# Attention steps on TensorE: the scores of the next two steps issued in front of the projections' parts instead of behind them

## The reference

```
xn = _layernorm(x, axis=-1)
x = x + _L0_attn_ref(xn, w_qkv, w_out) + _L0_ffn_ref(xn, wg, w1, b1, w2, b2)
...
scores = jnp.einsum('bhnqd,bhnkd->bhnqk', qb, k_kv) * scale      # 16 heads of 16, blocks of 64 queries x 128 keys
scores = jnp.where(_band_mask(nb), scores, NEG_INF)
attn = jax.nn.softmax(scores, axis=-1)
ob = jnp.einsum('bhnqk,bhnkd->bhnqd', attn, v_kv)
out = ob...reshape(B, L, D) @ w_out
```

## Time and profile before

| | |
|---|---|
| three runs | 757.99, 759.27, 761.73 us, median 759.27 |
| the profiled execution | 760.58 us, span 758.8 us |
| granted TensorE clock, mean | 0.949 of full speed |
| PE, PEld busy | 93%, 80% |
| DVE, ACT, POOL busy | 63%, 63%, 56% |
| attention | 461 to 759 us |

### The profile page before, as it was taken

The page is one execution under the profiler, slowest core; times in us unless marked ns, Lnnn a source line. Parts: engine busy times, 40 slices in busy tenths (PEclk is TensorE's granted clock), DMA queues, the critical chain, the costliest instruction groups (busy, mean ns, idle before and its releaser), DMA issues. The chain is left out here.

```text
span 758.8 us, 18403 instructions
## 1 busy us (share of the span) xinstructions
PE 705.8 (93%) x5816; PEld 603.4 (80%) x5817; DVE 481.7 (63%) x1774; ACT 480.2 (63%) x1508; POOL 427.7 (56%) x818
## 2 busy tenths in 40 slices
PE   6686799999999999999999997999999999999885
PEld 3364689898898988989889896788888878878664
DVE  7773243543425345253452524999999989999994
ACT  4640480834709357192561905998989989999891
POOL 4502560543605336153351303899999989999993
PEclk8875699999999999999999998999999999999897
DMA  9722231142311423123241013132333415141411
GB/s 314 277 77 77 87 104 58 62 138 83 110 56 60 140 76 114 54 74 125 76 124 42 0 43 108 35 91 85 96 96 85 121 53 141 37 120 36 115 57 42
DMA packets 52308, 69.95 MB, mean 92 GB/s; under 512 B 6672, under 2 KB 44816, under 8 KB 52240
## 3 DMA queue, kind: packets, MB, share of 16 engines
q1 hardware_dynamic: 45744, 52.31, 21.3%
q0 software_dynamic: 6144, 16.79, 8.0%
q10 hardware_dynamic: 352, 0.04, 0.0%
HBM read 47.75 MB, written 16.78 MB: 85 GB/s over the span
## 5 line engine op out<-in xcount | busy, mean ns | idle before, releaser
L1059 ACT ACTIVATE a_p<-a_p,a_nmax 128x128 f32<-128x128 f32 x512 | 198.6, 395 | 35.6 <-DVE a_nmax L1088 35.4
L990 POOL TENSOR_SCALAR a_p<-a_p,a_rsum 128x128 f32<-128x128 f32 x512 | 192.3, 391 | 18.8 <-DVE a_rsum L1096 16.5
L719 DVE TENSOR_TENSOR m_hl<-m_hf,m_hh 128x512 fp32r<-128x512 f32 x128 | 93.1, 727 | 100.3 <-ACT m_hh L676 100.3
L55 PE MATMUL m_psY<-m_w2h,m_hh 128*128 128x256 f32 x512 | 145.1, 283 | 0.0
L55 PE MATMUL m_psY<-m_w2l,m_hh 128*128 128x256 f32 x512 | 143.8, 281 | 0.0
L55 PE MATMUL m_psY<-m_w2h,m_hl 128*128 128x256 f32 x512 | 143.8, 281 | 0.0
L672 ACT ACTIVATE m_hf<-m_psF,b1T 128x512 f32<-128x512 f32 x128 | 88.4, 691 | 66.3 <-PE m_psF L55 52.1
L640 POOL CAST m_w2h<-raw 128x256 fp32r<-128x256 f32 x64 | 25.4, 396 | 175.8 <-PE m_psY L55 120.5
L1088 DVE CUSTOM_DVE_ANT_0 a_p<-a_psS,mask 128x128 f32<-128x128 f32 x512 | 116.6, 281 | 6.3 <-PE a_psS L1212 5.1
L55 PE MATMUL m_psF<-m_xh,w1h 128*128 128x512 f32 x256 | 103.6, 405 | 1.9 <-DVE m_xl L696 1.9
L55 PE MATMUL m_psF<-m_xh,w1l 128*128 128x512 f32 x256 | 102.1, 399 | 0.0
(11 more groups left out here) (186 smaller groups left out, 1363.1 us busy)
## 6 DMA issues: line engine op xcount, KB each, us to landing
raw<-in_L_ffn_w SPq DMA_DIRECT2D x16, 1024.0 KB, 5.3
y_scratch<-y SPq DMA_DIRECT2D x64, 128.0 KB, 1.7
n_xin<-in_L_attn_x SPq DMA_DIRECT2D x8, 512.0 KB, 7.4
xn_scratch<-n_xn SPq DMA_DIRECT2D x8, 512.0 KB, 7.6
a_res<-in_L_attn_x SPq DMA_DIRECT2D x8, 512.0 KB, 3.8
out<-a_res SPq DMA_DIRECT2D x8, 512.0 KB, 3.0
xnr<-xn_scratch SPq DMA_DIRECT2D x7, 512.0 KB, 5.1
b2b<-in_L_ffn_b SPq DMA_DIRECT2D x8, 128.0 KB, 4.8
```

The source lines that it names most:

```text
L55: last = pe.matmul(out, a, b, start=(n_start and i == 0), stop=(n_stop and i == n - 1))
L719: dve.tensor_tensor(hl[:, u // HC, u % HC, :], hf[:, u % FR, :], hh[:, u // HC, u % HC, :].bitcast(fp32), ALU.subtract).then_inc(hl_done, 1)
L990: pool.tensor_scalar(e, e, rsum[:, r, j:j + 1], 0.0, ALU.mult, ALU.add).then_inc(norm_done, 1)
L1059: act.activation(e, e, ACT.Exp, scale=-1.0, bias=nmax[:, r, j:j + 1], accum_out=sums[:, r, j:j + 1]).then_inc(exp_done, 1)
```

## The change

In `steps` of PE the two lines that issue the scores of steps t+2 and t+3 move from behind the projections' parts to in front of them. Nothing else changes; no instruction is added or removed, and the order on DVE, ACT, POOL and SP is the same as before.

```diff
                         ins.then_inc(pv_done, 1)
+                    if t % 2 == 0 and (t < BS - 2 or t == BS - 2 and not last):
+                        scores(b, t + 2, first)
                     if t < BS:
                         for i in range(NI):
                             parts = [part for item, part in parts_at[t % STEPS] if item == i]
...
                                 product(kind, j, 1 - u, count(b, u, i, first, last), i % 2,
                                         16 * (b * 2 + u + 2), (b * 2 + u) * (STEPS // GRP), parts)
-                    if t % 2 == 0 and (t < BS - 2 or t == BS - 2 and not last):
-                        scores(b, t + 2, first)
```

## The result

The changed kernel takes 782.71 us (median of 4, 780.97 to 784.49) against 760.50 (median of 4 of the kernel before, 757.99 to 763.94): a ratio of 1.029 with a 95% interval of 1.027 to 1.031. It is slower by 22 us; 777 was forecast, with a range of 766 to 791. The profiled execution takes 780.97 us, the shortest of the four, with a span of 779.2 us against 758.8.

A forecast was written before the change was run, and what follows sets the result against it. DVE and PE were both taken as full in the steady part, each idle moment on DVE adding time. 2.45 us in each of seven units gave 17.2, ramp and last unit zero: 777 us, range 766 to 791.

The forecast's parts named there:

- the clock's rival: New PE waits of 1.1 to 1.2 us make the granted clock fall once per unit: 787 us, chance 0.25.
- DVE has nothing to gain and pays each wait: Steady part: DVE does not wait for scores, so earlier ones win nothing; every idle moment put on DVE adds time.
- x, 0.4: Step 0: scores wait for DVE's last maximum, so x0 reaches ACT and DVE's a_xTl 0.4 us late per unit.
- k0, 0.3: Steps 2 to 4: k0's parts land behind the scores of step 4, and DVE reads k 0.3 us late.
- q1, 1.0: Steps 5 to 8: ACT gets q1 1.1 us late, and its exps delay DVE's reciprocal of step 8 by 1.0.
- v0, 0.45, and v2, 0.3: Steps 12 to 16: ACT reads v0 1.1 to 1.2 us late; 0.45 passes to DVE's reciprocal, v2 adds 0.3.
- o, nothing: Steps 8 to 11: DVE reads o one step later and is itself 1.7 us late, so no loss.
- The ramp, 0, between -2.3 and +3: First unit: gain from fewer DVE waits and loss from later q0 and k0, left at zero, bounds -2.3 to +3 us.
- Switching between kinds of tiles: Transposes directly before scores cost up to 0.23 us more in even steps: 0.3 per unit, 779; left out of the sum.
- Half of the walk: ACT and DVE run ahead in places and the reciprocal's wait is not reached: 1.2 us per unit, 768, chance 0.11.
- a shift paid once: PE falls behind DVE by one wait of 0.5 to 1.1 us, then never waits again: 760 us, chance 0.05.
- faster: Earlier scores feed a starved chain in the ramp and last unit: at most 3.7 us gained, 755.6, chance 0.04.

The follow-up runs named there:

- e4: Kernel before, with scores moved in front of the parts in steps 2, 8 and 10 alone: 770.83 us, ratio to before 1.0028.
- e1: Kernel before, with scores moved in front of the parts in step 6 of each unit alone: 773.89 us, ratio to before 1.0063.
- e5: Changed kernel, with ACT reading q1, v0 and v2 behind the step's exps instead of in front: 780.76 us, ratio to the kernel before 1.0160.
- e3: Kernel before, with scores moved in front of the parts in steps 0 and 4 alone: 776.22 us, ratio to before 1.0092.
- e10: Changed kernel, with the old order put back in step 2 of each unit: 790.30 us, ratio to the kernel before 1.0316.
- e12: e11 plus eight matmuls, their result overwritten, in front of the scores of step 12 to fill PE's wait: 775.21 us, ratio to the kernel before 1.0112.
- e2: Kernel before, with scores moved in front of the parts in steps 12 and 14 alone: 783.06 us, ratio to before 1.0176.
- e11: e2 run once more as the reference for e12: 780.41 us, ratio to the kernel before 1.0189.

## Why the prediction was right

The direction and the mechanism held, and the size in the main. The sum was 17.2 + 0 and the measured difference of the profiled spans is 20.4: 3.2 of the 5.7 us between 777 and 782.7. The other 2.5 come from the step to the median, for which the forecast took 1.3 off, rounded up by 0.5, while the median of the changed kernel lies 1.7 above its profiled execution. Their mean granted clocks are 0.947 (profiled), 0.947, 0.941 and 0.945, so some of that may be clock; no trace shows where.

Two things were luck. Within the unit the misses at x (0.4 too much) and q1 (0.4 too little) cancel, which is why 2.45 lies so near the measured 2.7. And by its number alone 782.7 is nearer to the clock's rival, 787, than to 777; it is the trace, with a granted clock of 1.00 in the units, that decides between them.

*DVE has nothing to gain and pays each wait.* Shown: the unit grew by 2.8 and DVE's idle time by 2.4 of it; e4 shows no gain from early scores in the steady units; e1 shows the loss where PE has no wait before the scores; e5 shows that 9.5 us of the loss go when ACT's order protects the reciprocal.

*x, 0.4.* Measured 0. The walk took DVE as punctual at step 0, but the reciprocal of step 0 is already 0.52 late, which covers it. Here one delay hides the next on the same engine. e3 shows it from the other side: its reciprocal of step 0 is on time, and DVE stands 0.36 before a_xTl, released by ACT, in three of its units (0.16 in two others), close to the 0.4 of the walk.

*k0, 0.3.* Measured 0.27.

*q1, 1.0.* Measured 1.41, the largest mis-sized term in the unit. The 0.96 on ACT before q1 is less than the 1.1 forecast, but the walk left out what ACT lost before it: 0.19 at q0 and 0.33 at the product with v, which had become late too. ACT had no room to make these up. Its three waits are 1.48 in all, DVE's two up to this reciprocal 0.27 + 1.41 = 1.68. The walk was right that the way from step 4's scores decides; my later theory of step 2 (e10) was not.

*v0, 0.45, and v2, 0.3.* Measured 0.51 and 0.52, with ACT 1.19 late at v0 where 1.1 to 1.2 was forecast; e12 has 0.52 and 0.54 with these steps alone.

*o, nothing.* DVE has no wait before a_res in the unit.

*The ramp, 0, between -2.3 and +3.* Measured +3.8 (6.5 less 2.7), outside these bounds, and the largest mis-sized term of the whole sum. DVE's waits there, 458 to 480 us, name it:

```profile
DVE a_p L1088 <- PE a_psS L1212: 3.8, 2, 2.7
...
DVE a_xTl L1070 <- ACT a_xTh L1017: 3.2, 2, 3.0
...
DVE a_pT L1103 <- PE a_psP L1226: 2.1, 1, 2.1
DVE a_k L1075 <- PE a_psA L1185: 1.5, 1, 1.5
```

The waits for x, transposed weights and k were 0.7, 0.9 and 0.5 before: 4.7 more. DVE's waits for scores fell from 5.1 to 3.8, the gain that the forecast had in mind, and the rest, 3.4, is most of the 3.8. x was made while PE waited for the first maxima anyway; now it comes behind them, at a lower clock (0.63 against 0.81 over the 18 us), and q0 behind it. I had the loss in mind and set it to zero for want of a row.

*Switching between kinds of tiles.* Four transposes before the scores take 0.53, the pair that no row of before showed:

```profile
594.95 0.60 PE L1226 MATMUL a_psP<-eye,a_p 128*128 128x128 f32 x4
595.48 1.16 PE L1212 MATMUL a_psS<-a_k,a_q 32*128 32x128 f32 x16
```

That is 0.17 above the 0.36 before parts. The bound of 0.23 from the v product was read from transposes that stood behind scores, so it holds two switches. Where the transposes stand behind parts, as after the change, they take the same 0.53 before the v product:

```profile
588.36 0.60 PE L1226 MATMUL a_psP<-eye,a_p 128*128 128x128 f32 x4
588.89 0.43 PE L1246 MATMUL a_psO<-a_pT,vs 128*32 128x128 f32 x8
```

The rule of the Trainium skill (page TensorEngine Tiling (Array Packing), section Key Properties) that changing the mode drains the engine agrees with it; on the way from step 4's scores to q1 the new pair lies once, in step 6.

*The rivals.* The clock did not fall in the changed kernel's steady part, so 787 was not reached, yet its mechanism is real: e2 has a fall in each of seven units and e11 in four. "Half of the walk" is refuted by the reciprocals, "a shift paid once" by units of 37.4 us one after another, "faster" by the steady units of e4. (e4's first unit is 34.0 us from x to x, against 34.5 before; with one trace of each that is not a measured gain.)

What stays open is what makes the clock fall. The length of the wait alone does not decide it: e11 loses the clock behind 1.27 and keeps it behind 1.30 and 1.33, with the same instructions in the same order. The changed kernel (both its traces) waits 1.25 in step 12 of six units and keeps it each time; it also has another wait of about 0.45 five microseconds earlier, which e2 and e11 lack, but no run varied that.

## What to carry to other kernels

Before an instruction is moved up an in-order queue, look at what it waits for, and count everything that now stands behind that wait: the instruction's own length plus the wait is added to each of them, and those whose readers have no room set the loss. Room is read between a reader's start and its producer's end, and on an engine that is full it is nothing. A delay can hide behind one that came just before it on the same engine, as x did, and small ones on the engine in between add up, as q0 and the product with v did on ACT; so walk them in order. A wait that you see grow may be a result: e5 halved PE's waits without touching PE.

## What the runs showed of the hardware

A wait of PE of 1.1 to 1.3 us can cost more than its length. In e2 and e11, 11 of 14 such waits were followed, 1 to 2 us after their end, by some 3.5 us at a granted clock of 0.50, at a price of 1.5 us per unit; three of 1.23 to 1.33 were not. With eight matmuls for nothing in its place the wait was 0.33, no fall came in any unit's step 12, and the kernel was 5.2 us faster. Four full-width transposes followed by 32-row matmuls, or by the product with v, take 0.53 us, against 0.36 followed by full-width ones.
